# Controller and router biases seeded into PSUM by ScalarE, input-norm sums moved from VectorE to ScalarE, all weight loads on one queue, and a new hand-written order

## The reference, cut to what matters

```
xn  = layernorm(x)
s   = recurrence(xn)                 # every second token
g   = silu(layernorm(moe_ffn(xn)))   # as used here: tokens in pairs, see below
out = x + s * g

recurrence: xs = rmsnorm(xn[:, ::2]) * g_norm
            x_proj, gate = split(xs @ w_in + b_in)
            h = tanh(h * A + x_proj[t][:, None] * B)     # 2048 steps, h is 4 x 512 x 64
            y = h @ sum(C) + Dv * x_proj[t]
            s = (y * silu(gate)) @ w_out + b_out, each row used for two tokens
moe_ffn:    spikes = sigmoid(xn @ W_enc + b_enc)          # 512 -> 1024
            cont   = spikes @ W_s2c + b_s2c               # controller, 1024 -> 64
            gates  = top 2 of 8 of softmax(cont @ Wr + br)   # router
            eo     = sum over 8 experts of gate * (relu(cont @ W1 + b1) @ W2 + b2)
            dec    = sigmoid(eo @ W_c2s + b_c2s) @ W_dec + b_dec
```

## Time and profile before

| | |
|---|---|
| median of three executions | 6132.56 us |
| the profiled execution, its own time | 6143.14 us |
| its span, first to last instruction | 6141.3 us |
| PE busy | 5782.2 us, 94% |
| DVE busy | 5633.2 us, 92% |
| POOL busy | 5300.8 us, 86% |
| ACT busy | 4209.2 us, 69% |
| mean granted TensorE clock | 0.985 of full speed |

### The profile page before, as it was taken

How to read it: one execution, slowest core, us unless ns; L and a number is a source line. 1 busy time by engine, 2 the same in 40 slices (tenths; PEclk the granted TensorE clock), 3 DMA queues, 4 the chain that set the end, 5 groups by cost and what they waited for, 6 DMA issues and landing times.

```text
span 6141.3 us, 87284 instructions
## 1 busy us (share of the span) xinstructions
PE 5782.2 (94%) x28640; PEld 3187.1 (52%) x28640; DVE 5633.2 (92%) x9556; ACT 4209.2 (69%) x8981; POOL 5300.8 (86%) x2828
## 2 busy tenths in 40 slices
PE   5999999999999999999999999999999999999998
PEld 3555555555555555555555555555555555555554
DVE  4999999999999989999999999999999999999997
ACT  3677676676776767667767667677676676676775
POOL 3888888888888878888888888888888988888887
PEclk9999999999999989999999999999999999999999
DMA  5444444444444444444444444444444444444443
GB/s 143 109 109 107 114 105 110 117 99 114 113 108 114 106 100 112 105 114 109 107 114 105 110 117 99 114 111 107 115 106 109 114 104 111 114 102 114 112 107 86
DMA packets 158073, 673.34 MB, mean 110 GB/s; under 512 B 45619, under 2 KB 46643, under 8 KB 92083
## 3 DMA queue, kind: packets, MB, share of 16 engines
q1 hardware_dynamic: 151488, 658.29, 44.5%
q10 hardware_dynamic: 6132, 9.47, 0.6%
HBM read 617.25 MB, written 50.33 MB: 109 GB/s over the span
## 4 chain that ended last, share of the span: by engine, by line
PE 39%; DVE 31%; ACT 18%; issue 11%; ACTq 1%; POOL 0%; DVEq 0%; DMA 0%; SPq 0%; POOLq 0%
DVE ps_z L1033 15%; PE bank L877 13%; ACT h L554 12%; DVE ps_z L1027 11%; PE ps_y L789 6%; PE ps_acc L889 5%; PE bank L809 4%; PE bank L950 4%; PE ps_acc L837 2%; ACT wide L582 2%; PE bank L863 2%; DVE g L1098 1%; DVE g L1113 1%; DVE conte L1107 1%; ACT squares L661 1%
## 5 line engine op out<-in xcount | busy, mean ns | idle before, releaser
L480 POOL TENSOR_TENSOR u<-xb,bt 128x1024 f32<-128x1024 f32 x2048 | 4811.0, 2361 | 469.1 <-DVE ps_z L1033 432.4
L554 ACT ACTIVATE h<-ps_z 128x512 f32<-128x512 f32 x4096 | 2418.0, 600 | 1375.6 <-DVE ps_z L1033 1358.0
L1027 DVE TENSOR_TENSOR ps_z<-h,ps_A 128x512 f32<-128x512 f32 x4096 | 2689.1, 692 | 376.0 <-ACT h L554 277.4
L1033 DVE TENSOR_TENSOR ps_z<-ps_z,u 128x512 f32<-128x512 f32 x4096 | 2666.4, 691 | 0.6 <-POOL u L480 0.6
L877 PE MATMUL bank<-wide,w 65*128 65x256 f32 x4096 | 1021.6, 393 | 0.4
L789 PE MATMUL ps_y<-h,c_wide 128*32 128x512 f32 x8192 | 987.1, 600 | 2.0 <-ACT h L554 2.0
L822 PE MATMUL bank<-xnT,w_enc 128*128 128x256 f32 x4096 | 911.4, 381 | 0.0
L877 PEld LDWEIGHTS bank<-wide,w 65*128 65x128 f32 x4096 | 741.4, 191 | 286.6 <-issue 154.6
L822 PEld LDWEIGHTS bank<-xnT,w_enc 128*128 128x128 f32 x4096 | 774.3, 190 | 181.4 <-issue 83.4
L809 PE MATMUL bank<-w_in,xnT 128*128 128x512 f32 x1024 | 468.4, 601 | 90.6 <-ACT xnT L572 90.6
L789 PEld LDWEIGHTS ps_y<-h,c_wide 128*32 128x32 f32 x8192 | 214.1, 109 | 531.3 <-issue 385.4
(11 more groups left out here) (117 smaller groups left out, 4373.9 us busy)
## 6 DMA issues: line engine op xcount, KB each, us to landing
xb<-x_proj_scratch SPq DMA_DIRECT2D x2048, 256.0 KB, 4.5
xbuf<-in_L_attn_x SPq DMA_DIRECT2D x256, 128.0 KB
xres<-in_L_attn_x SPq DMA_DIRECT2D x512, 64.0 KB
out<-g SPq DMA_DIRECT2D x256, 128.0 KB
x_proj_scratch<-xp SPq DMA_DIRECT2D x256, 64.0 KB
w_enc<-in_L_ffn_W_enc ACTq DMA_DIRECT2D x1, 2048.0 KB
w_dec<-in_L_ffn_W_dec ACTq DMA_DIRECT2D x1, 2048.0 KB
w_in<-in_L_attn_w_in SPq DMA_DIRECT2D x1, 2048.0 KB, 16.8
```

The source lines that it names most:

```text
L480: pool.tensor_tensor(u[:, tau % 2, :, :], xt, bt[:, :, :], ALU.mult).then_inc(u_ready, 1)
L554: act.activation(h[:, tau % RING, f, :], ps_z[:, f, :], ACT.Tanh).then_inc(h_ready, 1)
L1027: dve.tensor_tensor(ps_z[:, f, :], h[:, (tau - 1) % RING, f, :], ps_A[:, f, :], ALU.mult).then_inc(m_done, 1)
L1033: dve.tensor_tensor(ps_z[:, f, :], ps_z[:, f, :], u[:, tau % 2, f, :], ALU.add).then_inc(z_ready, 1)
```

## The change

What it does:

- `proj_stats`, `proj_aggr` and `proj_moments` go. ACT takes the sum of each half (a Copy of xbuf onto itself with accum_out, 128x512), the negated mean, the sum of squares about it (Square with bias, accum_out, 128x512), and two 128x2 instructions for the variance.
- The br_row matmul goes. A row set `acc_row` (controller bias in the first 256 columns, router bias differences behind) is prepared once, and ACT copies it into the whole bank ps_acc for each block (`acc_seed`, 128x512) as soon as the bank is drained; `contT_copy` is a plain copy.
- `run_bodies` walks 16 grains per step on every engine instead of 1 to 4, and nearly all slots have new values.
- All loads are issued by SP: first group, early group, then the store and first chunk of x_proj, then the late group, and only then the second chunk and the loop.
- The column sums at the start trade banks (ps_y and ps_acc). `scale_cont` waits in both halves, the squares have their scratch in hT.

```diff
+            load_early(...)            # 12 loads, now on SP, behind the first group
             store_scratch(0, 0)
             load_chunk(0, 0)
+            load_late(...)             # 9 loads, now on SP
...
-            pool.wait_ge(ready, 2)
             proj_scale(0)
...
+            def proj_sum(blk, q):
+                act.wait_ge(x_loaded, 16 * QUAD * (blk + 1))
+                act.activation(xbuf[:, q, :], xbuf[:, q, :], ACT.Copy, accum_out=p_sum[:, q:q + 1]).then_inc(p_sum_steps, 1)
+            def proj_mean(blk):
+                act.wait_ge(p_sum_steps, 3 * blk + 2)
+                act.activation(p_mean[:, :], p_sum[:, :], ACT.Copy, scale=-1.0 / D).then_inc(p_sum_steps, 1)
+            def proj_square(blk, q):
...
+                act.activation(squares_p, xbuf[:, q, :], ACT.Square, bias=p_mean[:, q:q + 1],
+                               accum_out=p_ss[:, q:q + 1]).then_inc(p_square_steps, 1)
+            def proj_var(blk):
...
+            def acc_seed(blk):
+                if not is_first(blk):
+                    wait_dec_drained(act, blk - 1, 1)
+                act.activation(ps_acc[:, :], acc_row[:, :], ACT.Copy).then_inc(acc_seeded, 1)
...
-                if not is_first(blk):
-                    wait_dec_drained(pe, blk - 1, 1)
-                pe.matmul(ps_acc[:, T2:T2 + 2 * (E * E + M)], ones[96:97, :], br_row, start=True, stop=True)
+                pe.wait_ge(acc_seeded, blk + 1)
...
-            def proj_stats(blk):
-                dve.wait_ge(x_loaded, 16 * QUAD * (blk + 1))
-                for q in range(2):
-                    dve.bn_stats(p_st[:, q, :], xbuf[:, q, :]).then_inc(p_stats_done, 1)
```

More of the change, by code:

```diff
@@ L33 @@
 STEPS = 32
+GRAIN = 16
 QUAD = 4
@@ L82 @@
[L82 to L99, removed]
@@ L352, in body @@
             def body(blk, par):
-                for n in range(STEPS * parts):
-                    slot = n / parts
-                    steps(blk, slot)
+                for n in range(STEPS * GRAIN):
+                    slot = n / GRAIN
+                    if n % (GRAIN // parts) == 0:
+                        steps(blk, slot)
                     if not is_first(blk):
@@ L360, in body @@
                         between(blk + 1, 1 - par, slot - STEPS)
-            body(0, 0)
-            for blk in range(1, LAST):
+            for blk in range(NB):
                 body(blk, blk % 2)
-            body(LAST, LAST % 2)
-            for n in range(STEPS * parts):
-                between(LAST, LAST % 2, STEPS + n / parts)
+            for n in range(STEPS * GRAIN):
+                between(LAST, LAST % 2, STEPS + n / GRAIN)
         def is_first(blk):
@@ L604, in contT_copy @@
                 act.wait_ge(contT_ready, blk + 1)
-                act.activation(contT, contT_acc, ACT.Identity, bias=cont_bias[:, :]).then_inc(contT_copied, 1)
+                act.activation(contT, contT_acc, ACT.Copy).then_inc(contT_copied, 1)
             def route_sig(blk):
@@ L734, in between @@
                         proj_evac(blk, par, q)
-                if slot == ACT_PROJ_MOMENTS:
-                    proj_moments(blk)
+                for q in range(2):
+                    if slot == ACT_PROJ_SUM[q]:
+                        proj_sum(blk, q)
+                if slot == ACT_PROJ_MEAN:
+                    proj_mean(blk)
+                for q in range(2):
+                    if slot == ACT_PROJ_SQUARE[q]:
+                        proj_square(blk, q)
+                if slot == ACT_PROJ_VAR:
+                    proj_var(blk)
                 if slot == ACT_GATE_SILU:
@@ L971, in _ @@
             for k in range(KH):
-                pe.matmul(ps_acc[0:M, 8:9], w_s2c[:, k, :], ones[:, 0:1], start=(k == 0), stop=(k == KH - 1))
+                pe.matmul(ps_y[0:M, 0:1], w_s2c[:, k, :], ones[:, 0:1], start=(k == 0), stop=(k == KH - 1))
             for k in range(KH):
-                ins = pe.matmul(ps_y[:, :], ones[:, :], w_dec[:, k, :], start=(k == 0), stop=(k == KH - 1))
+                ins = pe.matmul(ps_acc[:, :], ones[:, :], w_dec[:, k, :], start=(k == 0), stop=(k == KH - 1))
             ins.then_inc(columns_summed, 1)
```

200 lines of the change are left out of this document (111 added, 89 removed).

## The result

The changed kernel takes 5856.48 us (median of four runs, 5849.57 to 5866.21), the one before 6139.79 (four runs). The ratio is 0.9537, interval 0.9509 to 0.9565. The profiled execution took 5857.5, 285.6 less than the profiled one of before.

The account below looks back on a forecast made before the run. The chain DVE-tanh-DVE was taken to set the pace, PE only 4 us behind. From 6143.1, blocks took off 173, the start 27, the long drop 12, and the end added 1: 5932, given as 5930, range 5862 to 6045.

Parts of the forecast that it names:

- Norm's sums off DVE: VectorE's 1.59 us a block of norm sums, hidden by the controller's wait; removal alone gives about 0.1 a block.
- The controller's wait: ScalarE's 2.29 us wait for the controller goes with the copy one step later, releasing the 1.59 and 1.0 of remainder.
- New work on ACT: Sums, squares and seed add some 3.3 us a block on ScalarE; windows of steps 3 and 4 just fit, priced 0.
- The start: Loads before the loop: first group lands at 18, early group near 38, first step at 61; 27 us gained.
- rival 4: Next block's x lands too late for ScalarE's first sum; 5 us late gives 6250 us; chance 0.04.
- Sum of a block ... 91.2: Whole block after the change: steps 81.9, DVE's other work 6.0 and the stalls give 91.2 us, against 93.9 before.
- around step 9: Norm on ScalarE waits about 1.3 for POOL's proj_scale; tanh 0 comes 2.0 late, fin_mul covers, 0.85 us lost.
- DVE's other work: VectorE work in a block outside steps, norm sums, clock and stalls, taken as the remainder 93.9 - 87.9 = 6.0 us.
- relus between the tanhs: Three relus on ScalarE between a step's two tanhs, at 0.37 to 0.5 each, make 1.2 us a block.
- expert stretch: With relus spread, ScalarE waits for PE in four places by 0.1 to 0.2; stall 0.4 in place of 2.3 us.
- The clock: Reduced clock over the run: one long drop, about 12 us, assumed absent from the ordinary execution and subtracted from 5944.
- Rival 2: PE-bound, tightly packed, everything covered: 90.0 us a block and 30 at the start, 5851 us; chance 0.14.

Follow-up runs that it names:

- experiment 7: Kernel before with the norm's sums on ScalarE alone, controller's copy still in step 5: 6153.42 us beside 6154.08, ratio 1.0017.
- experiment 1: Changed kernel with the norm's mean and variance taken by VectorE again: 6032.32 us, ratio 0.9801 to the kernel before.
- experiment 6: Changed kernel with loads on ScalarE's queue, sums on VectorE and biases by PE again, leaving the new order: 6060.0 us, ratio 0.9824 to the kernel before.
- experiment 5: Changed kernel with early and late loads issued by ScalarE again, ahead of its first compute: 5901.03 us, ratio 0.9588 to the kernel before.
- experiment 11: Kernel before with one unread matmul more, filling most of PE's 1.33 us idle time: 6142.59 us, ratio 0.9988.
- experiments 8 to 10: Kernel before with controller's copy at 6.5: 6249.38 us; with sums on ScalarE too: 6200.42; with fin_mul also at 8.75: 6377.39.

## Why the prediction was right in direction and wrong in size

**Right.** *Norm's sums off DVE*: hidden in the old order (experiment 7, 0), 1.4 a block once the wait is gone (experiment 1). *The controller's wait*: gone, and the idle time ahead of the controller came out at 1.27 where 1.4 was said. *New work on ACT*: both windows just fit; no stall stands there, and experiment 6 shows the same stalls without that work. *The start*: 27 taken, 25.7 measured, though by two errors that cancel: the first group landed at 24.2, not 18, and the early group at 40.8, not 38, so that the first step came at 64.7, not 61. The chain behind took 23.8, near the 23.1 said, and step 4 was not held by the second chunk, for which 2 us had been kept. The Trainium skill, "DMA: Bandwidth & Descriptors", section "Issuing engines are not separate DMA queues", says that transfers issued by different engines interleave on shared engines; the first group, which lands at 34.6 before and 34.8 in experiment 5, with two issuers, and at 24.2 with one, agrees. The price of 10 us that was worked out beside it, for a late second chunk, did not come: SP issued that chunk at 58.8, and its issues cost no step. *Slower, the next x late* (rival 4): ScalarE waits for x once in the whole run, at the start.

**Wrong: "Sum of a block ... 91.2".** It is 89.8. The step that failed is this sum, in two of its terms: the stall "around step 9", 0.85, and the remainder, 6.0, "DVE's other work". Measured by how much longer than 2.56 each step lasts in the clean block shown (steps stay at 81.9 by construction):

| term | said | measured |
|---|---|---|
| relus between the tanhs | 1.2 | 1.14 (three at 0.38) |
| expert stretch | 0.4 | 0.63 (0.19, 0.09, 0.35) |
| around step 9 | 0.85 | 0.30 |
| gate write | 0.55 | 0.36 |
| square and conte | 0.3 | 0.16 (conte; square none) |
| DVE's other work | 6.0 | 5.3 |

The norm waits 0.69 for POOL, not 1.3, and fin_mul covers nearly all of it. The 6.0 was a remainder, into which whatever the other terms missed had gone: by the lengths of the steps the same items of DVE take 5.3 before too, and the stalls and the sums 6.2 together, not 3.9 + 1.6. The 3.9 had been taken from idle brackets, and one between a step's two multiplies leaves out 0.1 of what it costs.

The measured terms make 7.9; together the terms of the sum are 1.4 too high, 90 us over 64 blocks. The range's low end, a block of 90.2, leaves 2.3 for stalls beside the same 6.0; measured are 2.6 and 5.3, so it inherited the fault of the remainder. That put it 25 us too high by the block; 6 too low by the start (32 against 26) and 15 too low by the clock took most of this back.

**The clock** was priced by its one long drop (12). The half us for every second block was taken out of the block's parts but stood in none of the sum's terms: silently, the forecast had the short drops disappear. They did, in this kernel; experiments 1 and 6 show that nothing guaranteed it (25 and 23 blocks with a short drop alone came back with the sums on DVE). That the ordinary execution is without the long drop was an assumption; the kernel before varies by 76 us between executions, with the clock (experiment 11). What remained is 15 us in three long drops. By the sum with the measured terms, 6143.1 less 12 for the long drop of before, less 64 x (93.9 - 89.8) = 262, plus 15, less 26 at the start is 5858, and 5857.5 was measured.

**Rival 2** named the time (5851 by 90.0 a block and 30 at the start), but not the mechanism: PE still has 2.2 us idle and 0.86 of it can be filled for nothing. What paces the block is still DVE and tanh; 2.1 us of DVE's waits are left.

**Missed in experiments 8 to 10**: the later copy does take ScalarE's wait for the controller away, but time is gained only when all that depends on the controller's result has been moved as well. In the old order one local wait conceals the next, 1.63 at fin_mul, then 1.09 at the projection. The prediction, which gave 1.0 and 1.59 a block to the wait and the sums behind it, had not priced this; in the new order these places are moved too. The order is what pays (2.2 of 3.6 a block); the sums on ScalarE then pay 1.4; the seed pays nothing; the loads pay 26 to 30 once.

## What to carry to other kernels

A wait that hides other work must be removed together with what stands behind it: put into the old order, singly or two and three together, the parts gained nothing or lost up to 3%; the new order without them gained 1.8%, and with them 4.6%. Size a remainder ("all other work") from its rows before building a bound on it, measure a stall by the length of the step and not by the idle time alone, and give a stretch of reduced clock a term of its own on both sides of the sum. Where two orders differ by tenths of a us per block, time both: the clock can put 100 us between them.

## What the runs showed of the hardware

The granted clock falls to its lower level (1.2 GHz, 0.50 in the window 1012 to 1022) in stretches tied to a place in the block, and the place goes with the order of PE's work:

- *Short ones.* Before, stretches of 3.4 us begin 9 to 10 us behind fin_y, just behind PE's idle 1.33, which ends 8.2 behind it, in about every second block: 1.0 us each. Filling that idle time removes all of them (experiment 11). The changed kernel idles 1.27 in front of the same controller and has none in the 62 intervals ahead of the last; nor does one follow the 1.46 before the projection in the kernel before. With the sums on DVE they are back, at 14.5 to 15.2 us behind fin_y, and cost 1.2. There too they stand just behind an idle time of PE, which ends 14.3 behind fin_y and is 0.29 in the changed kernel (experiment 6, then the changed kernel):

```profile
2989.04 3.67 PE L958 MATMUL bank<-w_out,conte 128*128 128x512 f32 x8 [1.72 <-ACT bank L660]
```

```profile
2969.18 3.67 PE L991 MATMUL bank<-w_out,conte 128*128 128x512 f32 x8 [0.29 <-ACT bank L710]
```

- *Long ones.* In the changed kernel three stretches of 10.2 us all begin 36.0 us behind fin_y, in the transposes and expert matmuls, and cost 4.9 each; PE had been busy for the whole of the 5 us before the one shown. The old kernel's are 27.3 us long, begin some 37.5 behind fin_y and cost 13. Relus moved by half a step raise their number from 3 to 24, at the same place.

That the first kind goes when its idle gap is filled is shown for the old order only; for the gap of 1.7 no run fills it, and the length of a gap alone does not tell. What makes the second kind begin, and why so small a change of the order multiplies it, stays open: no run separates it from the order itself. What they cost is plain: 141 us lie between the profiled executions of the changed kernel and of the one with relus moved, of which 24 x 4.9 - 15 = 103 is clock.
